# Hybrid transformer block on one Trainium2 core: attention B with its shifted scores nine slots behind the maxima, and a reordered start, tail and end of that stage

## The chip, the cores and the metric

The kernel runs on one core of a Trainium2 chip. The metric is the device time of one execution in microseconds (us): the median of several executions. Engines: PE (TensorE), DVE (VectorE), ACT (ScalarE), POOL (GpSimd), SP (the queue that issues the DMAs here).

## The reference, cut to what matters

```python
x = x + attn_a(layernorm(x))            # 8 x 256 x 128, 16 heads of 8
x = x + ffn(layernorm(x))               # router, 64 experts by coefficients, one shared expert
x = x + attn_b(layernorm(x))            # the stage that the change is in
x = x + ffn(layernorm(x))
# attn_b, for each of the 8 samples and 16 heads:
q, k = rope(q), rope(k)
attn = softmax(q @ k.T / sqrt(8))       # 256 x 256
out = (attn @ v) @ proj_w.T + proj_b
```

## The kernel before, in words

The program of each engine is written out by hand, and the engines meet by semaphores. The work goes through attention A (up to about 330 us), the first expert layer (to 608 us), attention B (608 to about 812 us) and the second expert layer (to the end). Only attention B and the hand-over to the last layer are touched.

**Its preparation** (`prepare_b`, PE L854, ACT L1397, POOL L1696, DVE L2213) makes rotated q and k in four groups of 512 tokens. DVE computes the low parts of q and k (`lows_b`, L2236), PE spreads them over heads (`select_q_b`, L838; `select_k_b`, L847), ACT and DVE copy them out of PSUM. PE's program ends with the fourth group; around its `select_q_b` stand the scores of slots 0 and 1 (`b_tiles(-1, 0)`, `b_tiles(-1, 1)`) and fillers (`keep_busy`, L878: products into a PSUM bank that nobody reads).

**The slots.** There are 64 units (8 samples by 8 pairs of heads). In a slot V, PE computes the scores of a unit's two heads (`b_score_step`, two products of 256 columns a head) and DVE takes their row maxima (`head_max`, L2271). Three PSUM banks take the scores in turn, so the scores of a head wait for the maximum of the head three before it (`s_mx`). After four slots, a quad, POOL splits the maxima into two parts (`max_split`, L1711), PE transposes them in the second slot of the next quad (`b_max_transposed`, L949), ACT copies them, PE selects them in the third (`b_max_selected`), and DVE subtracts them from q (`shift`, L2281). In the same slot PE computes the shifted scores of unit U = V - AHEAD (`b_shifted_step`), where AHEAD is 8: keys against shifted queries. ACT takes the exponentials (L1439, two a slot), and PE multiplies them with the values (`pv_b`, eight products a slot). Two products of units go into one bank, and ACT copies it out after the exponentials of every fourth U (`copy_out`, L1421); the next `pv_b` into that bank waits for it. `samples_b` is the loop: slots 2 to 7 without a U, then U from 0 to 64; the slots from U = 56 on have no scores, and PE takes their two heads one after the other. `WAITS_FOR_PATH` and `TAIL_FILL` (L895, L896) say before which slots PE issues fillers.

**The path beside the slots.** Once a quarter of the heads is copied out, SP stores it to DRAM in four transfers (L511), waits for all of them, and loads it back by rows in four (L516). DVE divides by the sums (`normalise`, L2288 and L2292; after the maxima of slots 34 and 50, and once behind the loop), PE transposes (slots 35 and 51; U = 60) and projects, DVE adds the residual and takes the statistics, POOL normalises, PE transposes that for the router (`f_transposed`, L1084), ACT copies it and makes its high part (`copy_xT`, `f_high`), DVE its low part (`x_low`, L2015), PE computes router logits (`logits`), ACT their exponentials, DVE the sigmoids (L1931, L1932) and the routing. POOL adds the projection's bias to all of X once (L1732), as soon as the last normalised group of X is written.

**The end** (`last_of_b`, PE L1050): the last heads are transposed on the PE (L1007), normalised (L2300, L2303), projected, and the last 512 tokens go through the same path to the logits; DVE then routes the second half (from L1938 on), and PE's transposes of the coefficients (L1098) release the last expert layer.

Of the kernel before, what the change touches and what calls it, by code (L numbers as in the profile page):

```python
# [12 lines left out]
B, N = 8, 256  # L13
# [26 lines left out]
AHEAD = QUAD + 4  # L40
# [53 lines left out]
def hybrid(nc, x, consts, wA, wB, bqk, brow, rwT, wexp, out):  # L94
# [9 lines left out]
    with ctx:  # L104
# [219 lines left out]
        s_ost = sem("b_heads_stored")  # L324
# [94 lines left out]
        def _(sp):  # L419
# [88 lines left out]
            for c in range(CHUNKS - 1):  # L508
                sp.wait_ge(s_bev, 4 * (c + 1))
                for j in range(4):  # L510
                    sp.dma_start(o_d[c, j, :, :], o_all[32 * j:32 * j + VH, c, :]).then_inc(s_ost, 16)  # L511
                sp.wait_ge(s_ost, 64 * (c + 1))
                if c >= 1:
                    sp.wait_ge(s_on, B + c)
                for j in range(4):
                    sp.dma_start(b_rows[:, j, :, :], o_d[c, j, :, :].rearrange("x (p r) -> p x r", r=16)  # L516
                                 ).then_inc(s_old, 16)
# [19 lines left out]
        def _(pe):  # L537
# [316 lines left out]
            def prepare_b():  # L854
                keep_busy(0, 14)
                xn_transposed_b(0)
                project_b(0)
                values_b(0)
                xn_transposed_b(1)
                for g in range(GROUPS):  # L860
                    if g + 1 < GROUPS:
                        project_b(g + 1)
                    else:
                        pe.wait_ge(s_u, 2 * GROUPS)
                        pe.wait_ge(s_vc, 2 * GROUPS)
                        b_tiles(-1, 0)
                        keep_busy(2, 8)
                    select_q_b(g)
                    if g + 1 < GROUPS:
                        values_b(g + 1)  # L870
                    else:
                        keep_busy(2, 3)
                        b_tiles(-1, 1)
                    if g + 2 < GROUPS:
                        xn_transposed_b(g + 2)
                    select_k_b(g)
# [19 lines left out]
            TAIL_FILL = {56: 1, 57: 1, 58: 2, 59: 2, 60: 2, 61: 1, 62: 2, 63: 1, 64: 3}  # L896

            def b_tiles(U, V):
# [15 lines left out]
                if 0 <= U < 4:  # L914
                    keep_busy(shifted_bank(2 * U), 1)
                elif V in WAITS_FOR_PATH:
                    keep_busy(shifted_bank(2 * U), WAITS_FOR_PATH[V])
                elif U in TAIL_FILL:
                    keep_busy(shifted_bank(2 * U) if U <= 61 else 0, TAIL_FILL[U])
                for i in range(2):  # L920
                    if scores and 2 * V + i >= 3:
                        pe.wait_ge(s_mx, 2 * V + i - 2)
                    if shifted and i == 1 and U >= 1:
                        pe.wait_ge(s_e, 2 * U - 1)
                    for half in range(MT):
                        if scores:
                            last = b_score_step(V, half, i)
                            if half == MT - 1:
                                last.then_inc(s_s1, 1)
                        if shifted:  # L930
                            last = b_shifted_step(U, half, i)
                            if half == MT - 1:
                                last.then_inc(s_s2, 1)

# [45 lines left out]
            def samples_b():  # L980
                for V in range(2, AHEAD):
                    b_tiles(-1, V)
                    b_max_step(V)
                    keep_busy(3, 3)
                for U in range(B * UNITS + 1):
# [7 lines left out]
                    if U == B * UNITS - 1:  # L993
                        pv_b(B * UNITS // 2 - 2, 1)
                    elif U == 56:
                        pe.wait_ge(s_mx, 2 * B * UNITS - 1)
                        logits(1, 0, 0)
# [38 lines left out]
            def b_tail_step(U):  # L1036

                if U == 57:
                    pe.wait_ge(s_mx, 2 * B * UNITS)
                    logits(1, 0, 1)  # L1040
                elif U == 60:
# [5 lines left out]
                elif U == 62:  # L1047
                    projected(2, 1)

            def last_of_b():  # L1050
# [15 lines left out]
                keep_busy(4, 6)  # L1066
# [139 lines left out]
        def _(act):  # L1206
# [210 lines left out]
            def samples_b():  # L1417
# [14 lines left out]
                for U in range(B * UNITS + 3):  # L1432
                    C = U // 2
                    if U < B * UNITS:
# [6 lines left out]
                    if U == 57:  # L1441
                        logit_exps(1, 0, (0,))
# [4 lines left out]
                    if U in (27, 43):  # L1447
                        o_transposed_b((U - 27) // 16, 7)
                    elif U in (34, 50):
                        f_norm_rstd(1, (U - 34) // 16)  # L1450
                    elif U in (52, 56):
                        copy_xT((U - 52) // 4, 7)
                    elif U == 58:
                        logit_exps(1, 0, (1,))
                    elif U == 61:
# [4 lines left out]
            def copy_xT(g, n):  # L1460
                act.wait_ge(s_fxnT, GROUPS + g + 1)
                act.activation(f_xT[g][:, :], bank(n), ACT.Copy).then_inc(s_fxT, 1)
                act.wait_ge(s_fxT, GROUPS + g + 1)
                f_high(g)
# [22 lines left out]
            def last_of_b():  # L1487
                copy_xT(2, 7)
                o_transposed_b(3, 2)
# [124 lines left out]
        def _(pool):  # L1614
# [113 lines left out]
            def samples_b():  # L1728

                xb = X[:, :, :]  # L1730
                pool.wait_ge(s_xn, 2 * GROUPS)
                pool.tensor_tensor(xb, xb, pb_s[:, :].unsqueeze(1).broadcast_to([P, TILES, P]), ALU.add  # L1732
# [66 lines left out]
        def _(dve):  # L1799
# [466 lines left out]
            def samples_b():  # L2266
# [77 lines left out]
                marks(1)  # L2344
                sigmoids(1, 0, 0)
                x_low(1, 0, 1)
                shift(2 * B - 1)
                normalise(2)
# [175 lines left out]
```

## Time and profile before

| what | value |
|---|---|
| three executions | 1087.84, 1091.7, 1092.44 us; median 1091.7 |
| profiled execution, its own time | 1089.98 us |
| its span, first to last instruction | 1088.2 us |
| mean granted TensorE clock | 0.868 of full speed |
| attention B, first slot's maximum to last bank copied out | 647.1 to 780.1 us |
| last expert layer begins | 811.75 us |

Busy shares of an engine are averages over stages with other limits; the stage is read by the timeline, where each line gives a start in us from the span's beginning, the time in us, the engine, the line of the kernel, output and inputs, and in brackets how long the engine had been idle and who released it.

### The profile page before, as it was taken

The page shows a single profiled execution, that of the slowest core. Times are in us where ns is not written, and L with a number is a line of the kernel's source. Part 1 is how long each engine was busy: PE and PEld are TensorE (multiplying, and loading weights), DVE is VectorE, ACT ScalarE, POOL GpSimd, SP SyncE. Part 2 cuts the span into 40 slices and gives each one's busy share as a digit, 9 for nine tenths or more (in the row PEclk, how much of TensorE's full clock was granted, in tenths as well). Part 3 has the DMA queues.
Part 4 walks back from the last instruction along what each step waited for, and adds up shares of the span by engine and source line. Part 5 has one row for each costly group of instructions (what it writes and reads, how often), then busy time and mean ns, then how long its engine had stood idle before and what let it go on. Part 6 is the DMA issues. An engine that isn't in the chain of part 4 may idle for free. (4 is left out here: it accounts for less than half of the span.)

```text
span 1088.2 us, 17668 instructions
## 1 busy us (share of the span) xinstructions
PE 980.7 (90%) x5408; PEld 706.8 (65%) x5408; DVE 965.0 (89%) x1448; ACT 675.5 (62%) x855; POOL 374.6 (34%) x300
## 2 busy tenths in 40 slices
PE   6867888777669999999999889999989999999997
PEld 4633444444347888888888546555668888888885
DVE  7689999999988999999999788888789999999996
ACT  4679999999934454454454556776544454454553
POOL 2044666667901343343341131111113343343330
PEclk9765555555659999999999999999989999999999
DMA  2000000000108656555550000111149555555521
GB/s 59 1 1 1 1 1 1 1 1 1 52 20 206 174 147 154 156 141 160 151 147 15 1 1 1 23 24 20 26 98 235 157 146 157 154 142 161 150 72 39
DMA packets 50711, 86.94 MB, mean 80 GB/s; under 512 B 20092, under 2 KB 33404, under 8 KB 50556
## 3 DMA queue, kind: packets, MB, share of 16 engines
q1 hardware_dynamic: 50664, 86.34, 30.8%
q8 instruction: 27, 0.44, 0.2%
q14 instruction: 20, 0.16, 0.1%
HBM read 83.33 MB, written 2.98 MB: 79 GB/s over the span
## 5 line engine op out<-in xcount | busy, mean ns | idle before, releaser
L1535 ACT ACTIVATE sg<-ps 128x512 f32<-128x512 f32 x264 | 156.8, 594 | 265.4 <-PE ps L539 264.6
L539 PE MATMUL ps<-xh,whi 128*128 128x512 f32 x528 | 206.7, 391 | 1.3 <-ACT b L1357 1.3
L539 PE MATMUL ps<-xh,wlo 128*128 128x512 f32 x528 | 206.1, 390 | 0.0
L539 PE MATMUL ps<-xl,whi 128*128 128x512 f32 x528 | 206.0, 390 | 0.0
L2064 DVE TENSOR_TENSOR hf<-sg,ps 128x512 f32<-128x512 f32 x264 | 170.7, 684 | 30.5 <-DVE hl L2383 24.3
L1755 POOL CAST whi<-wraw 128x384 fp32r<-128x384 f32 x66 | 66.8, 1012 | 365.3 <-PE ps L539 285.4
L1675 POOL TENSOR_TENSOR rr<-xr,rr 128x2048 f32<-128x2048 f32 x32 | 145.3, 4577 | 126.8 <-ACT rr L1332 71.1
L2383 DVE TENSOR_TENSOR hl<-hf,hh 128x1024 fp32r<-128x1024 f32 x132 | 178.1, 1349 | 0.5 <-DVE hf L2064 0.5
L2388 DVE TENSOR_TENSOR hf<-hf,cbc 128x1024 f32<-128x1024 f32 x128 | 157.6, 1231 | 13.4
L1541 ACT ACTIVATE hh<-hf 128x1024 fp32r<-128x1024 f32 x132 | 139.1, 1054 | 4.6 <-DVE hf L2388 4.6
L1757 POOL TENSOR_TENSOR wlo<-wraw,whi 128x384 fp32r<-128x384 f32 x66 | 115.3, 1747 | 5.3
L539 PEld LDWEIGHTS ps<-xh,whi 128*128 128x128 f32 x528 | 99.5, 189 | 22.7 <-ACT b L1357 1.4
L539 PEld LDWEIGHTS ps<-xh,wlo 128*128 128x128 f32 x528 | 99.4, 188 | 21.0
L539 PEld LDWEIGHTS ps<-xl,whi 128*128 128x128 f32 x528 | 99.6, 189 | 20.7
L539 PE MATMUL ps<-hh,whi 128*128 128x512 f32 x264 | 104.4, 395 | 3.9 <-DVE hl L2383 3.9
L539 PE MATMUL ps<-hh,wlo 128*128 128x512 f32 x264 | 103.7, 393 | 0.0
L539 PE MATMUL ps<-hl,whi 128*128 128x512 f32 x264 | 103.6, 393 | 0.0
L2271 DVE TENSOR_REDUCE mx<-ps 128x2 f32<-128x512 f32 x128 | 81.8, 684 | 16.6 <-PE ps L539 15.7
L1439 ACT ACTIVATE wr<-ps 128x512 f32<-128x512 f32 x128 | 69.5, 595 | 31.2 <-PE ps L539 29.9
L2095 DVE TENSOR_SCALAR xr<-ps 128x1024 f32<-128x1024 f32 x64 | 77.9, 1216 | 10.3 <-PE ps L539 7.4
L539 PE MATMUL ps<-rr,vt 128*32 128x256 f32 x512 | 67.8, 634 | 17.2 <-ACT rr L1314 17.2
L2103 DVE SCALAR_TENSOR_TENSOR xr<-ps,xr 128x1024 f32<-128x1024 f32 x64 | 78.2, 1222 | 4.3 <-PE ps L539 0.3
(276 smaller groups left out, 1543.6 us busy)
## 6 DMA issues: line engine op xcount, KB each, us to landing
cbc<-routing_coefficients SPq DMA_DIRECT2D x256, 256.0 KB, 3.8
wraw<-in_wexp_dram SPq DMA_DIRECT2D x66, 192.0 KB, 2.8
X<-in_x_dram SPq DMA_DIRECT2D x4, 256.0 KB, 4.8
routing_coefficients<-cT SPq DMA_DIRECT2D x8, 128.0 KB, 2.3
out_dram<-X SPq DMA_DIRECT2D x4, 256.0 KB, 2.9
heads_by_row<-o_all SPq DMA_DIRECT2D x12, 72.0 KB
b_rows<-heads_by_row SPq DMA_DIRECT2D x12, 72.0 KB, 2.7
rope_in<-in_consts_dram SPq DMA_DIRECT2D x1, 512.0 KB, 3.4
```

Of the source, the lines that this page charges most:

```text
L539: return pe.matmul(o, l, r, start=start, stop=stop, **kw)
L1439: act.activation(wr[:, C % CHUNKS, h % 4 * MT * N:(h % 4 + 1) * MT * N], bank(shifted_bank(h)), ACT.Exp, scale=SCALE_B).then_inc(s_e, 1)
L1535: act.activation(sg[c % 2][:, :], bank(4 + 2 * (c % 2)), ACT.Silu).then_inc(s_sg, 1)
L1541: act.activation(hh[ring][:, :], hf[ring % 2][:, :], ACT.Copy).then_inc(s_hh, 1)
L1675: pool.tensor_tensor(rr[:, C % RR, :], xr[:, C % XR, :], rr[:, C % RR, :], ALU.add).then_inc(s_S, 1)
L1757: pool.tensor_tensor(wlo[slot][:, :], wraw[raw][:, :], whi[slot][:, :], ALU.subtract).then_inc(s_ws, 1)
L2064: dve.tensor_tensor(hf[c // 2][:, c % 2 * FF_TOK:(c % 2 + 1) * FF_TOK], sg[c % 2][:, :], bank(5 + 2 * (c % 2)), ALU.mult).then_inc(s_h1, 1)
L2095: dve.tensor_scalar(xr[:, C % XR, at], bank(0, 2), 0.0, None, ALU.max).then_inc(s_N, 1)
L2103: dve.scalar_tensor_tensor(xr[:, C % XR, at], bank(2, 2), R_MAX, xr[:, C % XR, at], ALU.min, ALU.mult).then_inc(s_X, 1)
L2271: dve.tensor_reduce(mx[U // UNITS % 2][:, c, j0 + i, :], bank(score_bank(2 * U + i)).rearrange("p (t m) -> p t m", t=MT), AX_X, ALU.max).t ...
L2383: dve.tensor_tensor(hl[ring][:, :], hf[ring % 2][:, :], hh[ring][:, :], ALU.subtract).then_inc(s_hl, 1)
L2388: dve.tensor_tensor(hf[side][:, :], hf[side][:, :], cbc[s][:, side * FF_PAIR:(side + 1) * FF_PAIR], ALU.mult).then_inc(s_h, 1)
```

## The change

`AHEAD` becomes 9: slots 3 to 8 stand ahead of the loop, 55 slots have both scores and shifted scores, nine have shifted scores alone. Slots 1 and 2 are scored by single heads around the last two selections. The PE's, ACT's and DVE's steps of the path keep their V; those that are counted by U are renumbered by one, and some change their place inside a slot. `...` marks what is left out.

```diff
-AHEAD = QUAD + 4
+AHEAD = QUAD + 5
...
-        s_ost = sem("b_heads_stored")
+        s_ost = [sem(f"b_heads_stored{j}") for j in range(4)]
...
                 for j in range(4):
-                    sp.dma_start(o_d[c, j, :, :], o_all[32 * j:32 * j + VH, c, :]).then_inc(s_ost, 16)
-                sp.wait_ge(s_ost, 64 * (c + 1))
+                    sp.dma_start(o_d[c, j, :, :], o_all[32 * j:32 * j + VH, c, :]).then_inc(s_ost[j], 16)
                 if c >= 1:
                     sp.wait_ge(s_on, B + c)
                 for j in range(4):
+                    sp.wait_ge(s_ost[j], 16 * (c + 1))
                     sp.dma_start(b_rows[:, j, :, :], ...).then_inc(s_old, 16)
...
# PE, prepare_b, last group
                         b_tiles(-1, 0)
-                        keep_busy(2, 8)
+                        keep_busy(3, 8)
+                        b_score_head(1, 0)
                     select_q_b(g)
...
-                        keep_busy(2, 3)
-                        b_tiles(-1, 1)
+                        b_score_head(1, 1)
+                        b_score_head(2, 0)
+                        b_score_head(2, 1)
...
-            TAIL_FILL = {56: 1, 57: 1, 58: 2, ... 64: 3}
+            TAIL_FILL = {55: 1, 56: 1, 57: 1, 58: 2, ... 64: 3}
# PE, b_tiles
+                if shifted and not scores:
+                    pe.wait_ge(s_e, 2 * U - 1)
+                    for half in range(MT):
+                        for i in range(2):
+                            last = b_shifted_step(U, half, i)
+                            if half == MT - 1:
+                                last.then_inc(s_s2, 1)
+                    return
...
+            def b_score_head(V, i):
+                if 2 * V + i >= 3:
+                    pe.wait_ge(s_mx, 2 * V + i - 2)
+                for half in range(MT):
+                    last = b_score_step(V, half, i)
+                last.then_inc(s_s1, 1)
# PE, samples_b and b_tail_step
-                for V in range(2, AHEAD):
+                for V in range(3, AHEAD):
...
-                    elif U == 56:
+                    elif U == 55:
                         pe.wait_ge(s_mx, 2 * B * UNITS - 1)
                         logits(1, 0, 0)
...
-                if U == 57:
+                if U == 56:
                     pe.wait_ge(s_mx, 2 * B * UNITS)
                     logits(1, 0, 1)
-                elif U == 60:
+                elif U == 59:
                     ...
                     transposed(2, 7)
                 elif U == 61:
                     pe.wait_ge(s_sc, lap(1, 0, 1))
-                elif U == 62:
                     projected(2, 1)
# PE, last_of_b
                 logits(1, 1, 0)
-                keep_busy(4, 6)
+                keep_busy(4, 12)
                 f_transposed(1, 1, 1)
# ACT, samples_b
+                    if U == 56:
+                        logit_exps(1, 0, (0,))
                     if U < B * UNITS:
                         ...
-                    if U == 57:
-                        logit_exps(1, 0, (0,))
...
-                    if U in (27, 43):
-                        o_transposed_b((U - 27) // 16, 7)
-                    elif U in (34, 50):
-                        f_norm_rstd(1, (U - 34) // 16)
-                    elif U in (52, 56):
-                        copy_xT((U - 52) // 4, 7)
-                    elif U == 58:
+                    if U in (26, 42):
+                        o_transposed_b((U - 26) // 16, 7)
+                    elif U in (33, 49):
+                        f_norm_rstd(1, (U - 33) // 16)
+                    elif U in (51, 55):
+                        copy_xT((U - 51) // 4, 7)
+                    elif U in (53, 58):
+                        act.wait_ge(s_fxT, GROUPS + 1 + (U - 53) // 5)
+                        f_high((U - 53) // 5)
+                    elif U == 57:
                         logit_exps(1, 0, (1,))
-                    elif U == 61:
+                    elif U == 60:
                         o_transposed_b(2, 7)
# (copy_xT no longer makes the high part itself; last_of_b does it for group 2)
# POOL, samples_b
                 pool.wait_ge(s_xn, 2 * GROUPS)
+                pool.wait_ge(s_lo, 2 * GROUPS)
                 pool.tensor_tensor(xb, xb, pb_s...)
# DVE, behind the loop of samples_b
                 x_low(1, 0, 0)
                 marks(1)
+                normalise(2)
                 sigmoids(1, 0, 0)
+                shift(2 * B - 1)
                 x_low(1, 0, 1)
-                shift(2 * B - 1)
-                normalise(2)
                 sigmoids(1, 0, 1)
```

## Rows read from the trace of the kernel before

**Rows 1.** The chain that ended last: start us, us, what.

```profile
644.27 3.01 issue
...
706.02 4.96 PE ps L539 x35
...
737.54 3.71 PE ps L539 x35
...
811.75 261.78 PE ps L539 x1148
```

**Rows 2.** Timeline, end of the preparation and first slots, POOL and DVE.

```profile
641.48 4.55 POOL L1732 TENSOR_TENSOR X<-X,pb_s 128x2048 f32<-128x2048 f32 x1
...
641.85 1.28 DVE L2246 TENSOR_SCALAR b_kt<-ps,kbias 128x1024 fp32r<-128x1024 f32 x1 [0.23 <-PE ps L539]
...
643.05 3.52 DVE L2236 TENSOR_TENSOR b_ql<-rope,b_qh 128x512 fp32r<-128x512 f32 x1
...
647.10 1.27 DVE L2271 TENSOR_REDUCE mx<-ps 128x2 f32<-128x512 f32 x2
...
650.72 6.55 DVE L2271 TENSOR_REDUCE mx<-ps 128x2 f32<-128x512 f32 x10 [2.35 <-PE ps L539]
```

**Rows 3.** Instructions of line 2236: duration in ns, least/median/most.

```profile
L2236 DVE TENSOR_TENSOR b_ql<-rope,b_qh x4: 660/691/3522, 620.8 to 643.1; 128x512 fp32r<-128x512 f32 x4
```

**Rows 4.** Busy time by stretch: PE, PEld, DVE, ACT, POOL (x), PEclk, DMA share, GB/s.

```profile
647.20:650.60 3.40, 3.32 (x21) 1.96 (x24) 1.18 (x2) 1.94 (x2) 0.00 (x0) 0.54 0.02 5
705.20:708.60 3.40, 3.40 (x16) 2.55 (x16) 1.05 (x2) 0.60 (x1) 0.70 (x4) 0.54 0.00 0
790.60:794.00 3.40, 2.65 (x9) 1.83 (x10) 3.26 (x6) 1.63 (x2) 3.24 (x4) 0.53 0.00 0
```

**Rows 5.** Timeline of one steady quad, ACT, PE and DVE.

```profile
684.02 0.61 ACT L1421 ACTIVATE o_all<-ps 128x512 f32<-128x512 f32 x1
684.77 0.64 PE L539 MATMUL ps<-wr,vt 128*32 128x256 f32 x8
...
689.13 1.29 DVE L2271 TENSOR_REDUCE mx<-ps 128x2 f32<-128x512 f32 x2 [0.53 <-PE ps L539]
```

**Rows 6.** Timeline, PE, a selection by two row groups in turn.

```profile
637.95 0.51 PE L539 MATMUL ps<-b_qh,sel 32*128 32x512 f32 x4
638.29 0.41 PE L539 MATMUL ps<-b_ql,sel 32*128 32x512 f32 x4
```

**Rows 7.** Timeline, PE, in the slots without scores.

```profile
761.13 0.47 PE L539 MATMUL ps<-sel 128*128 128x512 f32 x1
...
766.59 0.50 PE L539 MATMUL ps<-q,b_kt 32*128 32x256 f32 x4
767.02 0.64 PE L539 MATMUL ps<-wr,vt 128*32 128x256 f32 x8
...
777.42 0.97 PE L539 MATMUL ps<-sel 128*128 128x512 f32 x3
```

**Rows 8.** Timeline, DVE, in the same slots and just behind.

```profile
765.85 0.29 DVE L1931 TENSOR_SCALAR sc<-sc 128x256 f32<-128x256 f32 x1 [3.74 <-ACT sc L1471]
...
782.40 0.36 DVE L2300 RECIPROCAL b_rden<-ps 128x32 f32<-128x32 f32 x1 [0.23 <-PE ps L1007]
```

**Rows 9.** Timeline, SP, the last quarter stored and loaded back.

```profile
752.87 2.47 SPq L511 DMA_DIRECT2D heads_by_row<-o_all  x4
758.51 2.44 SPq L516 DMA_DIRECT2D b_rows<-heads_by_row  x4
```

**Rows 10.** Timeline, PE and DVE, router logits and start of the last routing.

```profile
786.34 1.00 PE L539 MATMUL ps<-rw_s,f_xT 128*128 128x64 f32 x8
...
793.58 1.97 PE L539 MATMUL ps<-rw_s,f_xT 128*128 128x64 f32 x8 [0.75 <-DVE f_xT L2324]
...
794.52 1.28 DVE L2015 TENSOR_TENSOR xl<-f_xT,xh 128x512 fp32r<-128x512 f32 x2
796.27 0.69 DVE L1938 TENSOR_TENSOR sfc<-sc,eb_s 128x512 f32<-128x512 f32 x1 [0.47 <-ACT sc L1515]
```

More of the change, by code:

```diff
@@ L895, in _ @@
             WAITS_FOR_PATH = {20: 3, 36: 4, 41: 3, 42: 4, 52: 4, 57: 3, 58: 4}
-            TAIL_FILL = {56: 1, 57: 1, 58: 2, 59: 2, 60: 2, 61: 1, 62: 2, 63: 1, 64: 3}
+            TAIL_FILL = {55: 1, 56: 1, 57: 1, 58: 2, 59: 2, 60: 2, 61: 1, 62: 2, 63: 1, 64: 3}
             def b_tiles(U, V):
@@ L1462, in copy_xT @@
                 act.activation(f_xT[g][:, :], bank(n), ACT.Copy).then_inc(s_fxT, 1)
-                act.wait_ge(s_fxT, GROUPS + g + 1)
-                f_high(g)
             def logit_exps(f, i, groups=range(2)):
@@ L1488, in last_of_b @@
                 copy_xT(2, 7)
+                act.wait_ge(s_fxT, GROUPS + 3)
+                f_high(2)
                 o_transposed_b(3, 2)
```

## The prediction, made before the changed kernel was run

> **What bounds the kernel now.** I read the chain of waits first: its last piece is the second expert layer, 261.78 us of back-to-back products from 811.75 on [rows 1]. The change touches nothing inside that layer, nor anything ahead of the fourth group's lows at 643. So the question is only by how much the layer's start, 811.75, moves. Then I read the timeline of attention B, in three parts.
>
> The start: the chain shows 3.01 us from 644.27 on in which PE does nothing [rows 1]. The reason stands on DVE: its low part of q, begun at 643.05, takes 3.52 us, while its median is 0.69 [rows 2, 3], and it ends soon after POOL's addition of the bias to all of X (641.48 to 646.03). The copy of k that DVE reads from PSUM lies inside the same addition and takes 1.28 us [rows 2]. What is held up is the instruction with both inputs in SBUF. Behind the idle time PE's granted clock falls to 0.54 in the mean of 647.2 to 650.6 [rows 4], i.e. mostly 1.2 in place of 2.4 GHz, and DVE stands idle 2.35 us before its third maximum [rows 2].
>
> The middle: DVE takes ten maxima in 6.55 us [rows 2], 0.655 each. A quad is eight of them and a shift at the same pace, some 5.8; DVE is idle 0.53 once a quad, waiting for PE [rows 5], so a quad lasts about 6.3. So PE and DVE bound it together by turns.
>
> The tail (U = 56 to 63): from the filler at 761.13 to that at 777.42, 16.3 us for eight slots [rows 7], without idle time on PE. The end behind it is a string of latencies through all engines up to the last routing, which begins on DVE at 796.27 [rows 10].
>
> **The start, part by part.** POOL's addition now waits for the fourth group's lows. The two lows then take 2 x 0.69 and end at 643.05 + 1.38 = 644.4 instead of about 647.2: **2.8 us** earlier, and PE's fillers, which last until 644.27, end as the selection becomes possible. The addition moves to about 644.4 to 649.0. Queued behind it on POOL is the first split of maxima; it needs the eighth maximum. With the first at 644.4, and no gap, the eighth ends at 644.4 + 8 x 0.655 = 649.6, so nothing waits. Beside the addition DVE only reduces from PSUM; the nearest row is that copy of 1.28 us, not held up, so I cost this at nothing (bounds: nothing, and 4.55 if the maxima were held for all of it).
>
> The heads of slot 1 and 2 are scored earlier: (1,0) ahead of the selection, three more between the selections, in place of three fillers and slot 1 as a whole. So the third maximum, at 650.72 before [rows 2], can follow the first two at 644.4 + 1.31 = 645.7. That is **5.0 us** earlier and contains the 2.8. From there on DVE has the same sequence to do as before, sixteen maxima and a shift to slot 9; PE's eight products of a selection take about 0.7, since four take 0.34 [rows 6], so the heads arrive in time if the clock stays high. The bounds are 2.8 (the heads give nothing) and 5.2.
>
> **Nine slots instead of eight.** The scores keep their pace, every U comes one slot later. One slot with both becomes one without scores at the end; the score-only slot at the start is in the sum already. A plain tail slot is a filler with its switch 0.4, shifted scores 767.02 - 766.59 = 0.43, values 0.57 to 0.64 [rows 7], together 1.45. Against it stands the order by turns: the two heads sit in different groups of 32 rows. The selections already alternate between two row groups: four products of 512 columns in 638.29 - 637.95 = 0.34 us [rows 6], 0.085 each, while four products of 256 columns of one head after the other take 0.43, 0.107 each [rows 7]. By columns that is a factor of 2.5; I take 2, hence 0.43 - 0.21 = 0.22 a slot, nine times 2.0. The Trainium skill (TensorEngine Tiling (Array Packing), Theoretical Speedup) has up to 4x for a small dimension of 32. By that rule the nine slots would save 0.32 each, 2.9 together; but it needs four row groups, and this change has two. Sum by the rows: +1.45 - 2.0 = -0.5. The new wait (both heads for the first exponential of the slot before) precedes the products; behind it stand that slot's values, and ACT pays only if its copies of the path are late. I take **-0.3**, with bounds +1.45 (turns buy nothing, since ACT or DVE is last) and -0.5.
>
> DVE must keep up. Its tail had idle times of 3.74 before the first sigmoid and 0.23 before the last division [rows 8]. With the tail 5.3 earlier the division is wanted at 777.1. `normalise` now fills the wait before the first sigmoid, and that sigmoid's exponentials stand ahead of a pair on ACT, about 1.1 earlier. But the second high part comes behind the exponentials of U = 58. Three slots at the tail's mean of 16.3 / 8 = 2.04, less 0.22 each and 0.3 more each for the logits they hold, put that slot at 761.13 - 5.0 + 6.4 = 762.5; its products, two exponentials and the high part (0.5, 1.2, 0.6: a copy of this size takes 0.61 [rows 5]) end at about 765.0. From there: low part 0.7, sigmoid 2.1, first routing 2.0, residual and statistics 1.9, groups and masks 4.4, i.e. 776.1. One microsecond of cover; if that is gone, it costs what is missing.
>
> **The middle.** Slots with both parts issue the same products in the same order. What rotates is ACT's copy-out: from the slot with the selection to the next, a short one. It now ends PE's wait in the second slot of a group of values instead of the first (before: copy 684.02 to 684.63, values at 684.77 [rows 5], a wait of about 0.2). The old wait goes, one of about the same size comes; bounds -0.1 and +0.2 a quad, over 13 quads -1.3 and +2.6. I take **0**.
>
> **SP.** The stores come one slot (1.6) later by the slots of the maxima; but a load no longer waits for all four stores. Before, the first load went out at 758.51, 5.6 behind the first store, and the four took 2.44 [rows 9]; now only the fourth can be that late, which gives back three quarters of 2.44, 1.8. Nothing on the path, cost **0**. No DMA is added. The weights' load waits for the last shift and moves with it.
>
> **The end.** Twelve fillers instead of six add 6 x 0.21 = 1.3 us to PE, in front of the wait for the last normalised tiles, which ends at 790.6, so they delay nothing. In the profile the clock falls just then (mean 0.53 over 790.6 to 794.0 [rows 4]), and the last logits take 1.97, against 1.00 for the same products at the full clock [rows 10]. If they keep the clock, the logits end 1.0 earlier, but DVE's low parts last until 795.80 and routing began at 796.27: **-0.4** (bounds 0 and -1.0).
>
> **Sum.** -5.0 - 0.3 + 0 + 0 - 0.4 = -5.7. The profiled execution took 1089.98, so 1084.3. The median of the three runs is 1.7 above it, and they lie 4.6 apart; I predict for the median 1085.0. About 0.5% (5.5 us) is what a measurement of this kernel can tell from no change, and my sum lies just on that line.
>
> **Rivals.**
> (a) The clock falls in the new start too. Between the selections PE waits for maxima, perhaps 0.9 of 2.2 us. For it: the 3.0 idle us were followed by the low clock, and so was PE's wait for the first normalised rows at 705 (0.54) [rows 4], though not the same wait at 737; the chain's piece behind it took 4.96 against 3.71 [rows 1]. Against it: these waits are short and apart. Then slots 3 to 5 run by PE at half speed, costing about 2, or more if the end falls as well (0.4): gain 3.0, time 1087.5.
> (b) The path's stalls at slots 35 and 51 stay at the full clock. This is the mirror of (a): another 1.2 to 1.4 gained, 1083.5.
> (c) The tail's chain over DVE is last and turns buy nothing: +1.45 instead of -0.3, gain 4.0, 1086.5.
> (d) Slower: the copy-out in the short slot holds PE each quad. It has about 0.2 of slack against DVE. From 0.44 a quad on (5.7 / 13) it eats the whole gain, from 0.86 on the kernel is slower by 0.5%, as at 1.0: 13.0 - 5.7 = +7.3, 1098. Against it: the copy lasts 0.61 and only moves by one slot [rows 5].
> (e) The reorder on POOL does not do what it says: the lows wait for something else at 643 (DVE's copy of k ends at 643.1 [rows 2]). Nothing in the rows is late enough, and it would leave 1089.
>
> **How the numbers follow.** The forecast (-5 to -7) has 0.48, (a) 0.20, (b) 0.12, (c) 0.12, (d) 0.04, (e) 0.04. Faster by over 0.5%: 0.6 of the forecast's 0.48, all of (b), and 0.09 of (a) and (c) by the scatter, 0.50. Slower 0.03 (most of (d)). The rest, 0.47, within 0.5%. The range runs from (b) with its bounds and the scatter of the runs, 1081, to the far end of (a), 1090.
>
> **What would show it.** Low q at 0.69, no idle 3 us on PE, POOL's addition from about 644.4 beside unhurt maxima; third maximum near 645.7; slot 9's near 656.9 (before 661.9); quads of 6.3; four shifted products within about 0.21; last routing near 790.6; last layer near 806. A granted clock under 0.9 between 644 and 656 would be (a); quads above 6.5 would be (d); maxima longer than 0.8 us beside POOL would make the first step wrong.

## The result, and the profile after

| | executions | median, us | range, us |
|---|---|---|---|
| before | 4 | 1089.77 | 1087.82 to 1092.44 |
| after | 4 | 1074.91 | 1074.57 to 1075.52 |

The ratio is 0.9863 (95% interval 0.9835 to 0.9891): 14.9 us faster, where 5.7 were forecast, and below the range of 1081 to 1090. The profiled execution took 1075.52, its span is 1073.7 us, and the mean granted clock 0.874 (0.868 before). The ratios here and below leave out executions that took over 1.5% longer than the fastest of the same kernel.

To compare kernels I cut each profile at six marks that all of them have. The first is the start of DVE's last copy of k, 641.85 in [rows 2]; its code and all code ahead of it are the same in all kernels. Then come POOL's maxima transposed on the PE in slots 5, 9 and 65 (L949 before, L967 after), the tail's first transposes to token-major (L1007, L1025) and the last transposes of the coefficients. The end of the span closes the table, which compares one execution of each kernel.

| stretch, us | before | after | after - before |
|---|---|---|---|
| up to the copy of k | 641.85 | 642.11 | +0.26 |
| start: to the transposes of slot 5 | 14.03 | 11.69 | -2.34 |
| slots 5 to 9 | 6.33 | 6.14 | -0.19 |
| middle: slots 9 to 65, fourteen quads | 102.65 | 91.64 | **-11.01** |
| tail: to token-major | 15.25 | 16.66 | +1.41 |
| end: to the last coefficients | 30.36 | 29.40 | -0.96 |
| last expert layer and output | 277.73 | 276.06 | -1.67 |
| span | 1088.2 | 1073.7 | -14.5 |

So the middle, which I had costed at nothing, is three quarters of it. Here is one slot of a steady quad of the changed kernel, slot 30, with the mark ahead of it, in the timeline of the PE (start, time, both in us, engine, line, output and inputs):

```profile
689.23 0.44 PE L967 MATMUL ps<-cst,mtok 128*128 128x128 f32 x2
689.60 0.38 PE L539 MATMUL ps<-b_kt,b_qt 32*128 32x256 f32 x1
689.60 0.38 PE L539 MATMUL ps<-q,b_kt 32*128 32x256 f32 x1
689.61 0.38 PE L539 MATMUL ps<-b_kt,b_qt 32*128 32x256 f32 x1
689.61 0.38 PE L539 MATMUL ps<-q,b_kt 32*128 32x256 f32 x1
689.82 0.27 PE L539 MATMUL ps<-b_kt,b_qt 32*128 32x256 f32 x1
...
690.04 0.64 PE L539 MATMUL ps<-wr,vt 128*32 128x256 f32 x8
```

The marks of the slots 21, 25, 29 and 33 stand at 677.74, 683.48, 689.23 and 694.98, so a steady quad is 5.75 us long; in the kernel before those of 21, 25 and 29 stood at 681.85, 688.11 and 694.37: 6.26. In the slot above four products start within 0.01 us, the other four 0.22 later, and the slot's values follow 0.44 us after the first. The slot in the same place of a quad of the kernel before, slot 22, also in the PE's timeline:

```profile
681.85 0.44 PE L949 MATMUL ps<-cst,mtok 128*128 128x128 f32 x2
682.22 0.39 PE L539 MATMUL ps<-b_kt,b_qt 32*128 32x256 f32 x2
682.44 0.29 PE L539 MATMUL ps<-q,b_kt 32*128 32x256 f32 x2
682.56 0.29 PE L539 MATMUL ps<-b_kt,b_qt 32*128 32x256 f32 x2
682.68 0.28 PE L539 MATMUL ps<-q,b_kt 32*128 32x256 f32 x2
682.89 0.64 PE L539 MATMUL ps<-wr,vt 128*32 128x256 f32 x8
```

They start two by two, 0.12 or 0.22 apart, and the values follow after 0.67. The products are the same, in the same order. What differs is the line `c, j0 = U % UNITS // 2, 2 * (U % 2)`: the two heads of a unit lie in the groups of 32 rows j0 and j0 + 1, groups 0 and 1 for an even unit, 2 and 3 for an odd one. With V - U = 8 the scores and the shifted scores of a slot always meet in the same two groups; with 9 always in different ones. Over the four slots of a quad, from the first of the eight products to the values, the times are 0.67, 0.88, 0.76 and 0.87 before and 0.44, 0.44, 1.34 and 0.44 after. The slot of 1.34 is held: between its two heads the next weights wait for DVE's maxima, and its values for the copy-out. The sum falls by 0.52, which is the whole difference of the quads.

The same sum of busy time shows it, over the same stretch, first before and then after (start:end, length, then busy time and number for PE, PEld, DVE, ACT, POOL, granted clock, DMA share, GB/s):

```profile
680.00:700.00 20.00, 19.62 (x220) 11.64 (x212) 18.05 (x30) 16.62 (x32) 2.09 (x12) 1.00 0.22 27
```

```profile
680.00:700.00 20.00, 17.46 (x221) 8.79 (x218) 19.42 (x32) 16.59 (x33) 2.10 (x12) 1.00 0.26 32
```

PE gets through as many products in 2.2 us less, at the same full clock, and DVE is now busy 19.42 of 20. The groups of this stretch by line and form show little idle time left ahead of the maxima (busy us, mean ns, then idle time ahead):

```profile
L2292 DVE TENSOR_REDUCE mx<-ps 128x2 f32<-128x512 f32 x26 | 16.4, 683 | 0.6
```

The chain does not name DVE in these quads. Each of them now holds two exponentials and the copy-out (ACT) beside the PE's pieces:

```profile
678.17 2.01 PE ps L539 x26
680.18 0.97 ACT wr L1458 x2
681.15 0.61 ACT o_all L1438
...
681.90 1.65 PE ps L539 x24
...
700.05 3.29 PE ps L539 x36
...
798.92 261.80 PE ps L539 x1148
```

So PE is no longer last throughout; whether DVE or the copy-out on ACT sets the 5.75 is not settled by this. The last layer begins at 798.92, against 811.75 [rows 1]. The pieces behind the path's transposes are 3.29 (700.05) and, at the second quarter, 3.30 (727.62); before they were 4.96, at a low clock, and 3.71 [rows 1, 4]. Hence the second part of the middle's gain: the first quad with the path took 10.29 us before and the one at the second quarter 8.83; after, both take 8.30. That difference, 1.46, is the low clock at 705, which is missing in this execution after the change. It is missing too in an execution of the kernel before with only POOL's wait added (experiment 7), where the same quad takes 8.82.

**The start** in the timeline of DVE, POOL and PE, which answers to [rows 2]:

```profile
642.41 3.27 PE L539 MATMUL ps<-sel 128*128 128x512 f32 x8
643.31 0.68 DVE L2257 TENSOR_TENSOR b_ql<-rope,b_qh 128x512 fp32r<-128x512 f32 x1
...
644.51 1.28 DVE L2292 TENSOR_REDUCE mx<-ps 128x2 f32<-128x512 f32 x2
644.74 4.54 POOL L1753 TENSOR_TENSOR X<-X,pb_s 128x2048 f32<-128x2048 f32 x1 [2.98 <-DVE b_kl L2257]
...
645.62 0.80 PE L539 MATMUL ps<-b_qh,sel 32*128 32x512 f32 x3
...
646.44 2.49 DVE L2292 TENSOR_REDUCE mx<-ps 128x2 f32<-128x512 f32 x4 [0.65 <-PE ps L539]
```

Low q takes 0.68 in place of 3.52, and the maxima beside POOL's addition are not held up (1.28 for two). But the eight fillers ahead take 3.27 us: low q is ready at 643.99, and the selection that waited for it before the change now starts at 645.62, behind them. The stretches behind run at a mixed clock (busy time by stretch, as above; the last row is from the end of attention B and answers to the third of [rows 4]):

```profile
641.50:645.00 3.50, 3.50 (x15) 2.53 (x16) 3.27 (x5) 1.49 (x3) 0.52 (x2) 0.72 0.02 5
645.00:648.50 3.50, 3.12 (x22) 1.70 (x20) 2.85 (x6) 1.73 (x2) 3.50 (x1) 0.79 0.00 0
648.50:652.00 3.50, 3.33 (x18) 2.05 (x17) 1.82 (x4) 3.48 (x4) 1.49 (x5) 0.70 0.00 0
...
784.00:788.00 4.00, 4.00 (x16) 3.29 (x15) 3.73 (x24) 3.21 (x5) 0.00 (x0) 0.70 0.30 70
```

**The tail and the end**, timelines of PE and DVE, against [rows 7, 8, 10]:

```profile
764.11 0.50 PE L539 MATMUL ps<-q,b_kt 32*128 32x256 f32 x4
764.54 1.07 PE L539 MATMUL ps<-wr,vt 128*32 128x256 f32 x16
...
769.51 0.36 DVE L2321 RECIPROCAL b_rden<-ps 128x32 f32<-128x32 f32 x1 [0.88 <-PE ps L1025]
...
781.28 1.10 PE L539 MATMUL ps<-rw_s,f_xT 128*128 128x64 f32 x8 [1.61 <-DVE f_xT L2345]
...
783.43 0.68 DVE L1959 TENSOR_TENSOR sfc<-sc,eb_s 128x512 f32<-128x512 f32 x1
```

Four shifted products by turns take 0.43 us (764.11 to 764.54), as they did one head after the other (766.59 to 767.02 [rows 7]). The last logits take 1.10 instead of 1.97, and the last routing begins at 783.43. But the last logits take 1.10 also in the profiles of experiments 3 and 4, which have the old end with six fillers.

### The profile page after: what moved, and what is told of

It reads as the page before. It is cut to its first block and busy times, and to the rows that moved or that the text cites. A ratio compares the mean times of both kernels' runs of the same rounds, so it can differ in the third digit from the quotient of the medians.

```text
span 1073.7 us, 17673 instructions
## 1 busy us (share of the span) xinstructions
PE 966.3 (90%) x5412; PEld 691.5 (64%) x5412; DVE 961.0 (89%) x1448; ACT 673.3 (63%) x855; POOL 375.6 (35%) x300
## 5 line engine op out<-in xcount | busy, mean ns | idle before, releaser
L539 PE MATMUL ps<-rr,vt 128*32 128x256 f32 x512 | 67.1, 628 | 17.3 <-ACT rr L1331 17.3
```

Source lines behind the costliest of these rows:

```text
L539: return pe.matmul(o, l, r, start=start, stop=stop, **kw)
```

## The experiments

The theory after the result (T): the parity of the lead is the gain; V and U in different pairs of row groups let four products run at once. Its main rival (R): the lead of nine itself, by its longer lead time or the rotation of the copy-out, or the other edits. The two come apart by exchanging the row groups: with `j0 = 2 - j0` for the scores alone, the lead of nine meets in the same groups, and the lead of eight in different ones. All expectations stand as they were written before the run.

**1. The changed kernel, rows made the same.**

```diff
             def b_score_step(V, nt, i):
                 s, c, j0 = unit_b(V)
+                j0 = 2 - j0
# DVE, head_max
-                    c, j0 = U % UNITS // 2, 2 * (U % 2)
+                    c, j0 = U % UNITS // 2, 2 - 2 * (U % 2)
```

The scores of an even unit then use the heads of row groups 2 and 3 and those of an odd one 0 and 1, while the shifted scores use the old ones; each unit's heads change places with its neighbour's, maxima in step.

> The changed kernel, with only the order of the two units inside a chunk swapped for scores and maxima, so that a slot's scores and shifted scores use the same two groups of 32 rows again, as before the change. Theory T (row groups): a lead of nine puts the two in different pairs of row groups, so PE runs four products at once, and that made the quads 5.75 instead of 6.26 us; here they go back to about 6.3, and the time rises by about 10 to 11 us, to about 1085. Rival R (the lead or the place of the copy-out in the quad did it): the quads stay at 5.75 and the time at 1075.

Measured: 1111.70, 1110.46, 1111.43 and 1078.93 us. In the profiled one, the first, the clock stood at half speed for about 65 us (0.64 over 660 to 680, 0.50 over 680 to 720, 0.74 over 720 to 740) in the middle of attention B. Two stretches, first inside it and then behind it:

```profile
680.00:700.00 20.00, 20.00 (x133) 10.85 (x135) 10.88 (x17) 9.31 (x19) 1.41 (x8) 0.50 0.00 1
...
744.00:757.00 13.00, 12.45 (x144) 7.31 (x144) 11.37 (x20) 10.07 (x21) 3.16 (x12) 1.00 0.39 47
```

In the second, the quad from the mark of slot 45 to that of slot 49 lasts 6.41 us at the full clock, so the lead of nine does not bring the quad of 5.75 by itself. The low clock ends ahead of the mark of slot 37, and from there to the mark of slot 65 the clock is full, in the PE's timeline:

```profile
732.67 0.44 PE L968 MATMUL ps<-cst,mtok 128*128 128x128 f32 x2
...
785.88 0.44 PE L968 MATMUL ps<-cst,mtok 128*128 128x128 f32 x2
```

These seven quads take 53.21 us, and in the changed kernel 48.30 (703.28 to 751.58): 4.9 us for the two edited lines, in half of the middle. That speaks for T. The total does not: three times are far above what T forecasts, and 1078.93, at a mean clock of 0.880, is 6 below it.

**2. The same, once more.** The same kernel again, to see whether the low clock was an accident.

> The kernel of changed_same_rows once more, for a profile at the full clock: there the clock stayed at half speed for 65 us of attention B, and only the quad of slots 45 to 48, 6.41 us, was at full clock. T (row groups): quads of 6.3 to 6.4 in all of the middle, and 9 to 11 us more than the changed kernel, 1084 to 1086. R: the 6.41 was chance, quads of 5.75, 1075.

Measured: 1110.79, 1111.06, 1110.61 and 1091.60; the same low clock in the same stretch, and a quad of 6.41 at the full clock. It was no accident. The seven quads from slot 37 take 53.23 here. Whether T explains the whole time difference stays open in this direction.

**3. The kernel before, rows made different.** The same two lines put into the kernel before, and nothing else.

> The kernel before, lead of eight, with only the same swap, so that a slot's scores and shifted scores use different row groups. T: quads of about 5.75, eight shifted products plus scores start within about 0.45 us instead of 0.67 to 0.88, the time falls from 1090 by about 9 to 11 us, to about 1080. R: quads stay at 6.26, the time at 1090.

Measured: 1082.64 us (1079.12 to 1085.56, seven executions), ratio 0.9948 (0.9929 to 0.9966). The quads, by the same marks:

```profile
684.73 0.44 PE L950 MATMUL ps<-cst,mtok 128*128 128x128 f32 x2
...
690.38 0.44 PE L950 MATMUL ps<-cst,mtok 128*128 128x128 f32 x2
```

5.65 us, where the kernel before has 6.26. The middle goes from 102.65 to 94.95, by 7.7, with a low stretch of the clock at the first path in both (that quad takes 10.29 and 9.48). With two lines and the old lead the quad is as short as after the change, even 0.1 shorter. T holds for the quad. The medians differ by 5.4 only (1088.08 for the kernel before, measured beside it), less than the middle alone and less than the 9 to 11 that T forecast; the profiled execution, 1079.12, was the fastest of the seven. The mean clock of its executions was 0.866 to 0.873, of the kernel before 0.868 to 0.876 (without the one of 1115.59), so part of it may have gone to more low clock; that is not shown.

**4. The kernel before, with a lead of nine and the same rows.** `AHEAD = QUAD + 5`, the path's steps renumbered as in the change, and the exchange of rows, so that the pairs meet as before.

> The kernel before with a lead of nine (its steps counted by U moved with it) and the units of a chunk swapped for scores and maxima, so that both products of a slot keep the same row groups; start, tail order and end are the old ones. It asks for the lead alone. T (row groups do it): quads of 6.3 to 6.4 where the clock is full, time that of the kernel before or 1 to 3 us more, unless the clock stays low as in changed_same_rows. R (the lead does it): quads of 5.75.

Measured: 1091.7 us, the median of ten executions, two of them at 1117.4 and 1119.0, the others 1088.17 to 1095.78; ratio 1.0021 (1.0004 to 1.0039). A slot and the wait of the quad, in the PE's timeline:

```profile
686.43 0.44 PE L950 MATMUL ps<-cst,mtok 128*128 128x128 f32 x2
...
688.48 0.39 PE L539 MATMUL ps<-b_kt,b_qt 32*128 32x256 f32 x2
...
689.15 0.64 PE L539 MATMUL ps<-wr,vt 128*32 128x256 f32 x8
...
691.03 0.64 PE L539 MATMUL ps<-wr,vt 128*32 128x256 f32 x8 [0.28 <-ACT o_all L1422]
...
692.84 0.44 PE L950 MATMUL ps<-cst,mtok 128*128 128x128 f32 x2
```

Two by two again, 0.67 from the first product to the values (0.44 in the changed kernel), and a quad of 6.41: 0.15 more than before, with a wait of 0.28 for the copy-out. So the lead of nine alone is worth nothing, or slightly less. R falls. Its start ran 20 us at the low clock, so only its middle is comparable: 101.37, against 101.19 at a lead of eight with the same rows and no low clock (experiment 7), and against 91.64 after the change, where the rows differ. The last difference is 9.7, the price of the row groups at a lead of nine.

**5. The changed kernel, with the lead of eight back and other rows.** All other edits stay.

```diff
-AHEAD = QUAD + 5
+AHEAD = QUAD + 4
             def b_score_step(V, nt, i):
                 s, c, j0 = unit_b(V)
+                j0 = 2 - j0
...
```

(and each step that is counted by U one later, as in the kernel before)

> The changed kernel with the lead put back to eight (steps counted by U put back with it) and the units of a chunk swapped for scores and maxima, so that the row groups differ. T: quads stay at 5.75 us; one plain slot of about 1.45 us less in the tail and one score-only slot less in front: 1073 to 1075. R (the lead did it): quads of 6.26, about 1084.

Measured: 1075.29 us (1074.78 to 1076.48), ratio 0.9881 (0.9851 to 0.9911), the changed kernel's time. Quads 5.66, tail 15.23 where the nine slots have 16.66; it gives that back in the middle (93.15 against 91.64), where each quad behind one with the path's transposes is longer (7.29 against 6.86). In its steady quads of 5.66 DVE still has 0.18 idle, so DVE alone does not set them.

**6. The order by turns taken out** of the changed kernel.

```diff
-                if shifted and not scores:
-                    pe.wait_ge(s_e, 2 * U - 1)
...
-                    return
```

> The changed kernel without the branch that takes the two heads by turns in the nine slots without scores. In the trace of the changed kernel four shifted products take 0.43 us there, as before. If turns buy nothing, the time stays at 1074.9 within 0.5; the prediction's step would have it 2.0 us slower.

Measured: 1076.28 us (1074.52 to 1080.97), ratio 0.9883 (0.9851 to 0.9914), not to be told from the change. The tail is 16.67 against 16.66. One head after the other, in the PE's timeline:

```profile
768.89 0.51 PE L539 MATMUL ps<-q,b_kt 32*128 32x256 f32 x4
769.32 1.07 PE L539 MATMUL ps<-wr,vt 128*32 128x256 f32 x16
```

0.43 from the first to the values, the same as by turns. The order buys nothing. That the profiled execution took 1080.97 is not the order either: it spent 9.90 us from slot 5 to slot 9, where the code is that of the changed kernel (6.14), at a clock of 0.50 from 650 to 662.

**7. Only POOL's wait**, in the kernel before.

```diff
                 pool.wait_ge(s_xn, 2 * GROUPS)
+                pool.wait_ge(s_lo, 2 * GROUPS)
```

> The kernel before with only POOL's wait for the fourth group's lows ahead of the addition of the bias. Prediction's step: low q takes 0.69 in place of 3.52 us, the first maximum comes 2.8 us earlier, and the whole time is 2.8 shorter (1.3 to 4 with the clock's part). If the preparation's other chains are last instead, under 1 us.

Measured: 1083.42 us (1080.68 to 1086.07), ratio 0.9957 (0.9939 to 0.9974), 5.0 less than the 1088.42 of the kernel before, measured beside it. DVE's and POOL's timeline:

```profile
641.38 0.68 DVE L2237 TENSOR_TENSOR b_ql<-rope,b_qh 128x512 fp32r<-128x512 f32 x1
...
642.58 1.28 DVE L2272 TENSOR_REDUCE mx<-ps 128x2 f32<-128x512 f32 x2
642.81 4.56 POOL L1733 TENSOR_TENSOR X<-X,pb_s 128x2048 f32<-128x2048 f32 x1 [2.98 <-DVE b_kl L2237]
...
646.10 1.29 DVE L2272 TENSOR_REDUCE mx<-ps 128x2 f32<-128x512 f32 x2 [2.24 <-PE ps L539]
```

Low q at 0.68 from 3.52, and the start 11.16 instead of 14.03: 2.87 us for one wait. The selection itself starts only 2.2 earlier, since its fillers take 3.03 in place of 2.11; the rest comes with the clock behind it, 1.00 from 645 to 653, where before it was 0.57 from 647 to 651. The third maximum begins at 646.10, 5.92 behind the copy of k; in the changed kernel, with its heads early, at 646.44, 4.33 behind. The remaining 2 us of the medians are not in this stretch. In the profile the middle was 1.5 shorter too (101.19), without its low clock, and 1.7 stand ahead of the copy of k, where the code is the same. The Trainium skill (SBUF — State Buffer, "SBUF: two separate sides") has DVE and GpSimd arbitrate for one port pair, exclusively and for a whole instruction, and names DVE operations with two SBUF inputs against a GpSimd operation that reads SBUF. The trace agrees: the subtraction of two SBUF operands took 3.52 beside the addition and 0.68 without it, and the two reductions from PSUM took 1.28 beside it.

**8. The old order of slots 1 and 2** in the changed kernel.

```diff
-                        keep_busy(3, 8)
-                        b_score_head(1, 0)
+                        keep_busy(2, 8)
...
-                        b_score_head(1, 1)
-                        b_score_head(2, 0)
-                        b_score_head(2, 1)
+                        keep_busy(2, 3)
+                        b_tiles(-1, 1)
```

> The changed kernel with the old order of slots 1 and 2 around the last selections. Prediction's step: the early heads bring the third maximum 2.2 us nearer, so the time rises by 2.2 without them. Against it: before_bias_later, with the old order, needed 11.2 us from the last copy of k to slot 5's transposes, the changed kernel 11.7; by that the time stays as it is, or falls.

Measured: 1075.62 us (1073.08 to 1081.88), ratio 0.9896 (0.9856 to 0.9936). The start takes 11.19, against 11.69 with the heads early. The early heads did bring the third maximum forward (experiment 7 against the change), but by slot 5 nothing was left of it. So they are worth nothing at the end of the start; its gain is POOL's wait. They may even cost something. In all eight profiles with the early heads the clock was low for part of 646 to 660, and from the copy of k to slot 9 they took 17.5 to 22.0, five of them over 20. The two profiles with POOL's wait and the old order (experiments 7 and 8) had the full clock from 646 to 657 and took 17.5 and 17.3, though experiment 8 had a low stretch behind that. Why the clock falls there is not shown.

**9. Six fillers instead of twelve at the end.** `keep_busy(4, 12)` becomes `keep_busy(4, 6)` in the changed kernel.

> The changed kernel with six fillers instead of twelve ahead of the last normalised tiles. Prediction's step: the clock falls earlier there, the last logits take up to 1.97 in place of 1.1 us, and the time rises by 0.4. A rival: the clock falls a little later anyway, no difference.

Measured: 1075.86 us (1074.89 to 1080.92), ratio 0.9903 (0.9874 to 0.9931). The end takes 29.92 instead of 29.40, with some 6.8 us at the low clock instead of 3.4. That is not shown to be the fillers: the end took 29.92 in experiment 6 too, with all twelve, and 29.39 in experiment 4 with six. Over all profiles it took 29.35 to 29.96 with twelve and 29.39 to 30.37 with six.

**10. Fewer fillers in the tail.** With other rows PE has become shorter than the rest, so its fillers may have turned into a load. Kernel 5 with all fillers of the tail but the last three removed:

```diff
-            TAIL_FILL = {56: 1, 57: 1, 58: 2, 59: 2, 60: 2, 61: 1, 62: 2, 63: 1, 64: 3}
+            TAIL_FILL = {64: 3}
```

> The kernel of lead_eight_other_rows without the fillers of U = 56 to 63 (13 fillers, about 0.24 us each on PE, which never stands idle there). If PE bounds the tail and keeps its clock: 2 to 3 us less, 1072.5. If DVE's chain bounds it, about the same; if the clock falls in the tail, up to 5 us more.

Measured: **1070.64 us** (1069.32 to 1072.29), ratio 0.9841 (0.9824 to 0.9858). It beats both kernels: its executions lie below all of the changed kernel's (1074.57 to 1075.52), though the two intervals of the ratio overlap. The tail takes 13.42, 1.8 less than kernel 5. The fillers taken out were twelve, not the thirteen of the expectation (the one of U = 55 is only in kernels with a lead of nine); at 0.24 each that is 2.9 us, and part of it is now waiting for the exponentials, 0.57 here and 0.27 two slots later, in the PE's timeline:

```profile
754.66 0.50 PE L539 MATMUL ps<-q,b_kt 32*128 32x256 f32 x4 [0.57 <-ACT wr L1459]
```

The clock stayed at full speed in spite of these waits:

```profile
750.00:764.00 14.00, 13.11 (x134) 7.29 (x127) 10.64 (x29) 10.87 (x23) 2.03 (x3) 1.00 0.14 43
```

The medians differ by 4.65; in the profiles the tail is 1.8 of 3.7, and 1.4 stand ahead of the copy of k, where the code is the same. So about half of that gain is in the stretch where the fillers stood.

**11. No fillers in the slots at all.** Kernel 10 with `WAITS_FOR_PATH = {}` too.

> The kernel of lead_eight_no_tail_filler without the fillers of slots 20, 36, 41, 42, 52, 57 and 58 too (25 fillers). If these slots are PE's: 2 to 5 us less, 1066 to 1069. If DVE or the path is last there: the same 1070.6. If the clock falls: more, up to 1075.

Measured: 1073.36 us (1069.31 to 1074.81), ratio 0.9843 (0.9815 to 0.9872). The middle shortens from 92.61 to 89.63, but slots 5 to 9 take 8.73 instead of 6.61, the last layer and output 277.62 instead of 276.09, and the clock's mean is 0.865 to 0.872. No further gain in the medians. The two stretches that got longer have no edit: slots 5 to 9 took as long (8.92, 9.90) in the profiles of experiments 9 and 6, which have these fillers. So the 3.0 of the middle stand in one profile, and the low clock elsewhere is not shown to be their price.

## Why the prediction was wrong

It had the sign, the wait on POOL and the copy-out right. It missed the largest term, and the gains of the early heads and of the turns were not there.

- **The middle, taken as 0, measured -11.0.** The step that failed is "Slots with both parts issue the same products in the same order." That is true, and it was taken for the whole answer. The same products in the same order run in 0.44 instead of 0.67 us when they meet in four groups of 32 rows instead of two. About 9.7 of the 11.0 are this (experiment 4 against the change; 7.7 at a lead of eight, experiment 3), and some 1.5 the clock at the first path, which was rival (b) and came true in this execution.
- **The evidence was at hand, and misread.** The four products of 512 columns in 0.34 us [rows 6] were taken for two row groups in turn. `select_half` takes two row groups, but these four are both of its halves, one product in each of the four groups, and all four start at 637.95. The selections of k, one half at a time, show the price of one half (PE's timeline of the kernel before):

```profile
639.80 0.50 PE L539 MATMUL ps<-b_kh,sel 32*128 32x512 f32 x2
640.14 0.40 PE L539 MATMUL ps<-b_kl,sel 32*128 32x512 f32 x2
```

Two products over two groups take 0.34, as long as four over four. So the factor of 2.5 holds no gain of an order by turns; it compares other shapes and other numbers of products a group. It was applied to nine slots of the tail and not to the 55 slots with both parts, where nothing is edited. I cited the Trainium skill (TensorEngine Tiling (Array Packing), Theoretical Speedup) with up to 4x for a dimension of 32, and wrote that "it needs four row groups, and this change has two". The change has four, by the parity of its lead, in every slot that has both parts. The trace agrees with the direction: eight products over four groups take 0.44, over two 0.67, a factor of 1.5 for twice the groups.
- **Quad 6.26 to 5.75, and not shorter.** Three of the four slots give back 1.1 us together, and the held slot takes 0.6 more. DVE's work of eight maxima and a shift, some 5.8 by my own reading, turned out a little smaller: a quad of 5.66 still had 0.18 of idle time on DVE (experiment 5). From a bound "by turns" of PE and DVE I could have had most of the size at once, had I asked what becomes of the idle 0.53 [rows 5]: 0.5 in each of fourteen quads is 7.
- **The copy-out's rotation**, bounds -0.1 and +0.2 a quad: +0.15 with the same rows (6.41 against 6.26), +0.09 with other rows (5.75 against 5.66). Inside the bounds; my 0 was a little kind. Rival (d) is dead.
- **POOL's addition, 2.8: right** (2.87, experiment 7), with some luck in the number: the selection came 2.2 earlier, for the fillers ahead of it ran at a low clock, and the rest was a clock that did not fall behind it. Rival (e) is dead.
- **The heads of slots 1 and 2, 2.2: wrong**, nothing (experiment 8). The third maximum came at 646.44 (forecast 645.7, before 650.72), yet slot 9's mark, counted from the copy of k, only 2.5 us earlier than before: the clock fell from the fillers on, and the lead was lost by slot 5. Rival (a) came true in this stretch, whose clock was under 0.9 as its sign asked.
- **The turns, -2.0: wrong**, 0 (experiment 6). The tail measured +1.41, which is the +1.45 of one more plain slot with nothing against it, as in rival (c), though not for its reason: DVE kept its idle time before the division (0.88). The factor that I took from the selections was not one of order.
- **SP, 0: right.** `normalise(2)` waited 3.39 us for the load, and the division behind the loop had 0.88 to spare.
- **The end, -0.4 with a bound of -1.0:** -0.96, the far bound, but not shown to be the twelve fillers: with six, experiments 3 and 4 also had the last logits at 1.10 and gained 0.5 and 1.0 there. That the number fell inside the bounds is luck. And the last stretch gave 1.67 that no part of the change touches: before, its clock was 0.69 at 1076 to 1080 and after 1.00. That belongs to the executions, not to the edit.

By its own sum, then: -5.0, -0.3, 0 and -0.4 were forecast for the start, the tail, the middle and the end; measured were -2.5, +1.4, -11.0, -1.0, and -1.4 outside the change.

What stays open: the share of the whole time. In the medians the rows alone brought 5.4 (experiment 3) and POOL's wait alone 5.0 (experiment 7), 10.4 of the 14.9; the rest is assigned by single profiles. Also how much of the clock's differences (1.5 at the path, 1.7 at the end) belongs to the change and how much to the four executions; and the time of the changed kernel with the same rows but without its long low clock, for which only 1078.93 and 1091.60 stand.

## What to carry to other kernels

When two kinds of small products share a slot, look at the groups of rows that they use, and at what the distance between them does to these: an odd lead instead of an even one, or one exchanged index, was worth 8 to 10 us of the middle here (5.4 in the medians, by itself), and no line of the slot had to change. Count the products that each row group gets in a slot. Once such a change shortens an engine, size its fillers again: without those of the tail that stretch was 1.8 us shorter, and its clock stayed full. And a term taken as 0 because "the same instructions are issued" deserves the question where they run, not only which and when.

## What the runs showed of the hardware

- **The clock can stay at half while PE has no idle time.** Six of the eight executions of experiments 1 and 2 took 1110.5 to 1111.7, the other two 1078.93 and 1091.60; in the two profiled ones the clock was 0.50 over 680 to 720, with PE busy 20.00 of each 20 us. Two of ten executions of experiment 4, and one of 36 of the kernel before (1115.59), show times of the same kind. All these kernels have scores and shifted scores in the same pair of row groups; none of the 35 executions with different pairs was above 1085.56. That is an association, the kernels differ in more, and all six executions of experiment 7, with the same pairs, were below 1086.1. What keeps the clock low is not settled. PE was not idle, at any rate. The Trainium skill (TensorE: Matmul & The Clock Gate, Seeing it yourself) calls the clock's trace records unreliable and tells of a clock seen stuck at a quarter for over 50 us; these runs show one at half for about 65, and here the record is borne out by the longer times.
- **Row groups, not order, decide.** At the full clock and for products of 32 rows and 256 columns, four over two row groups take 0.43 us, by turns and one head after the other (experiment 6); eight take 0.67 over two groups and 0.44 over four. By products a group: two products in each group take 0.43 over two groups and 0.44 over four, and four in each take 0.67.
- **Fillers did not always help.** Eight fillers between 642.41 and 645.68 in the start of the changed kernel took 3.27 us, partly at the low clock, and the selection behind them started 1.6 us after its input was ready.
